# Sparse attention and FP4 feed-forward on one core: the exponentials of a score pair split into two, each score bank signalled by itself

## The reference

```
h = layernorm(x) * (1 + ca) + sa
x = x + ga * attention(h)
h = layernorm(x) * (1 + cb) + sb
x = x + gb * ffn(h)          # fp4_linear(silu(fp4_linear(h, gate)) * fp4_linear(h, up), down)

# attention: 16 heads of 32 features, 4 sequences, so 64 heads in all
top_idx = top_k(norm(Q), 409)          # only the 409 longest queries of a head attend
scores  = Q[top_idx] @ K.T / sqrt(32)  # 409 x 2048
out[top_idx] = softmax(scores) @ V     # every other row is zero
return out @ Wo.T + bo
```

## Time and profile before

| | |
|---|---|
| median of 3 runs | 3447.15 us (3444.97 to 3452.52) |
| the profiled execution | 3417.03 us |
| its span, first to last instruction | 3415.1 us |
| mean granted clock of PE in it | 0.976 |
| busy: PE, PEld | 3216.7 us (94%), 1493.7 us (44%) |
| busy: DVE, POOL, ACT | 2582.2 us (76%), 1541.0 us (45%), 1109.4 us (32%) |
| scores (L1414), first to last start | 736.8 to 1670.2 us |

### The profile page before, as it was taken

How to read it: one execution, slowest core, us unless ns; L and a number is a source line. 1 busy time by engine, 2 the same in 40 slices (tenths; PEclk the granted TensorE clock), 3 DMA queues, 4 the chain that set the end, 5 groups by cost and what they waited for, 6 DMA issues and landing times.

```text
span 3415.1 us, 49956 instructions
## 1 busy us (share of the span) xinstructions
PE 3216.7 (94%) x16716; PEld 1493.7 (44%) x16716; DVE 2582.2 (76%) x3868; ACT 1109.4 (32%) x1538; POOL 1541.0 (45%) x1358
## 2 busy tenths in 40 slices
PE   7989989869999999999679999999999999999998
PEld 3544444423333333333235555555555555555554
DVE  4656758746666666666368989989998998999895
ACT  6751212226666666666311111111111111111111
POOL 4431222345565555555234444444445444444442
PEclk9999999979999999999889999999999999999999
DMA  6755448636333333232201110010011001001000
GB/s 225 251 185 157 128 127 251 179 85 210 104 86 109 91 94 114 81 82 81 92 19 32 31 31 28 31 31 31 28 34 31 28 31 31 31 28 34 31 19 16
DMA packets 203080, 282.19 MB, mean 83 GB/s; under 512 B 59508, under 2 KB 115188, under 8 KB 202228
## 3 DMA queue, kind: packets, MB, share of 16 engines
q1 hardware_dynamic: 186616, 274.42, 26.4%
q0 software_dynamic: 16384, 6.76, 1.1%
HBM read 169.36 MB, written 111.71 MB: 82 GB/s over the span
## 4 chain that ended last, share of the span: by engine, by line
PE 47%; DVE 1%; issue 1%; POOL 1%; DMA 0%; ACT 0%; SPq 0%; POOLq 0%; DVEq 0%
PE f_g L1924 4%; PE f_u L1924 4%; PE f_u L1923 4%; PE f_u L1925 4%; PE f_g L1925 4%; PE f_g L1923 4%; PE f_d L1946 4%; PE f_d L1947 4%; PE f_d L1945 4%; PE f_t L1935 2%; PE f_w L1902 2%; PE f_w L1903 2%; PE f_w L1904 2%; PE f_t L1911 1%; PE f_w L1896 1%
## 5 line engine op out<-in xcount | busy, mean ns | idle before, releaser
L1231 DVE TENSOR_REDUCE top<-ps_max 128x1 f32<-128x1024 f32 x384 | 463.2, 1222 | 232.6 <-PE ps_max L1376 231.7
L1319 ACT ACTIVATE p<-ps_exp,p_bias 128x820 f32<-128x820 f32 x512 | 482.9, 943 | 370.1 <-PE ps_exp L1414 364.5
L1195 POOL DMA_INDIRECT o_d<-o_rows,chosen x256 | 249.0, 973 | 344.8 <-DVE o_rows L1266 275.3
L1425 PE MATMUL ps_out<-p,v_tok 128*33 128x410 f32 x2048 | 403.2, 515 | 0.0
L1856 ACT ACTIVATE silu<-f_g 128x512 f32<-128x512 f32 (+1 forms) x192 | 107.8, 562 | 798.3 <-PE f_u L1925 798.3
L1414 PE MATMUL ps_exp<-q_exp,k_exp 98*128 98x410 f16 x1024 | 268.0, 344 | 43.6 <-ACT p L1319 43.5
L1174 POOL DMA_INDIRECT q_sel<-q_d,chosen x256 | 244.0, 953 | 79.6 <-issue 62.7
L1923 PE MATMUL f_g<-gu,xT_hi 128*128 128x512 f16 (+1 forms) x768 | 277.5, 361 | 1.0 <-DVE xT_lo L1661 1.0
L1924 PE MATMUL f_g<-gu,xT_hi 128*128 128x512 f16 (+1 forms) x768 | 277.5, 361 | 0.0
L1925 PE MATMUL f_g<-gu,xT_lo 128*128 128x512 f16 (+1 forms) x768 | 277.5, 361 | 0.0
L1924 PE MATMUL f_u<-gu,xT_hi 128*128 128x512 f16 (+1 forms) x768 | 277.5, 361 | 0.0
(11 more groups left out here) (241 smaller groups left out, 6609.8 us busy)
## 6 DMA issues: line engine op xcount, KB each, us to landing
k_max<-k_d SPq DMA_DIRECT2D x192, 128.0 KB, 3.0
k_exp<-k_d SPq DMA_DIRECT2D x192, 128.0 KB, 2.6
v_d<-v SPq DMA_DIRECT2D x16, 1056.0 KB, 9.4
v_tok<-v_d SPq DMA_DIRECT2D x64, 264.0 KB, 2.7
x<-in_x SPq DMA_DIRECT2D x16, 1024.0 KB, 9.1
q_d<-q SPq DMA_DIRECT2D x16, 1024.0 KB
a_in<-o_d SPq DMA_DIRECT2D x64, 256.0 KB, 2.6
f_x<-in_x SPq DMA_DIRECT2D x64, 256.0 KB, 2.6
```

Of the source, the lines that this page charges most:

```text
L1195: pool.indirect_dma_start(o_rows, bass.IndirectOffsetOnAxis(ap=con["chosen"][0:n, t, h:h + 1], axis=0), o_rows_of[u][0:n, t, :], None).the ...
L1231: ve.tensor_reduce(top[:, t, half:half + 1], ps[:, :, :].rearrange("p a n -> p (a n)"), AX.X, ALU.max, negate=True).then_inc(max_done, 1)
L1319: act.activation(p32[k % PB][:, :, :], ps_exp[:, :, 0:NQ], ACT.Exp, bias=con["p_bias"][:, 0:1], scale=scale).then_inc(p_done, 1)
L1425: last = pe.matmul(ps_out[at:at + VCOLS, 0:NQ], v_tok[u][:, t, :], p32[k % PB][:, s, :], start=k == 0, stop=k == STEPS - 1)
```

## The change

Every count of `s_ready` and `p_done` goes from one a step to two a step, one for each bank. `scores` waits, before each of its two matmuls, until the exponential of the same bank of the step before is done, and signals each matmul by itself. `exponentials` issues two instructions of 410 columns, each behind the signal of its own bank, and signals each by itself. `weigh` waits for both halves. The waits of SP, DVE and ACT at the head's end count accordingly and stand for the same events as before. No instruction is moved past another, and nothing outside these functions is touched.

```diff
@@ load_k_exp (SP), queries_again (DVE), take_top (ACT), each the same edit @@
-                    need(sp, s_ready, h * STEPS - STEPS)
+                    need(sp, s_ready, h * TILES - TILES)
...
@@ exponentials (ACT) @@
                 def exponentials(i, k):
-                    act.wait_ge(s_ready, i * STEPS + k + 1)
                     need(act, pv_done, i * STEPS + k - PB + 1)
-                    act.activation(p32[k % PB][:, :, :], ps_exp[:, :, 0:NQ], ACT.Exp, bias=con["p_bias"][:, 0:1],
-                                   scale=scale).then_inc(p_done, 1)
+                    for s in range(PER):
+                        act.wait_ge(s_ready, i * TILES + k * PER + s + 1)
+                        act.activation(p32[k % PB][:, s, :], ps_exp[:, s, 0:NQ], ACT.Exp, bias=con["p_bias"][:, 0:1],
+                                       scale=scale).then_inc(p_done, 1)
@@ scores (PE) @@
-                    need(pe, p_done, i * STEPS + k)
                     for s in range(PER):
-                        at = (k * PER + s) * P
-                        last = pe.matmul(ps_exp[:, s, 0:NQ], k_exp[u][:, at:at + P], q_exp[u][:, :], start=True, stop=True)
-                    last.then_inc(s_ready, 1)
+                        c = k * PER + s
+                        need(pe, p_done, i * TILES + c - PER + 1)
+                        pe.matmul(ps_exp[:, s, 0:NQ], k_exp[u][:, c * P:(c + 1) * P], q_exp[u][:, :], start=True, stop=True)\
+                          .then_inc(s_ready, 1)
@@ weigh (PE) @@
-                    pe.wait_ge(p_done, i * STEPS + k + 1)
+                    pe.wait_ge(p_done, i * TILES + k * PER + PER)
```

More of the change, by code:

```diff
@@ L1251, in queries_again @@
                     ve.wait_ge(qsel_done, h + 1)
-                    need(ve, s_ready, h * STEPS - STEPS)
+                    need(ve, s_ready, h * TILES - TILES)
                     ve.tensor_copy(q_exp[u][0:KROWS, :], q_max[u][:, :]).then_inc(qexp_done, 1)
@@ L1312, in take_top @@
                     act.wait_ge(rows_ready, h + 1)
-                    need(act, s_ready, h * STEPS - STEPS)
+                    need(act, s_ready, h * TILES - TILES)
                     act.activation(q_exp[u][KROWS:KROWS + 2, :], ps_misc[0:2, 0:NQ], ACT.Copy).then_inc(rows_done, 1)
                 def exponentials(i, k):
-                    act.wait_ge(s_ready, i * STEPS + k + 1)
                     need(act, pv_done, i * STEPS + k - PB + 1)
-                    act.activation(p32[k % PB][:, :, :], ps_exp[:, :, 0:NQ], ACT.Exp, bias=con["p_bias"][:, 0:1],
-                                   scale=scale).then_inc(p_done, 1)
+                    for s in range(PER):
+                        act.wait_ge(s_ready, i * TILES + k * PER + s + 1)
+                        act.activation(p32[k % PB][:, s, :], ps_exp[:, s, 0:NQ], ACT.Exp, bias=con["p_bias"][:, 0:1],
+                                       scale=scale).then_inc(p_done, 1)
                 def take_output(h):
```

## The result

| | before | changed |
|---|---|---|
| median of 6 runs each, side by side | 3449.8 us (3444.97 to 3453.74) | 3462.7 us (3460.21 to 3465.36) |
| ratio, with its 95% interval | | 1.0039 (1.0026 to 1.0052) |
| the profiled execution | 3417.03 us | 3460.89 us |
| scores, first to last start | 736.8 to 1670.2 us | 731.2 to 1713.3 us |

The change makes the kernel slower by 0.4%, 13 us. The forecast was 3401 us, faster by 46. The two profiled executions differ by 44 us, three times as much as the medians: the one that the prediction was made from is 33 us faster than the median of its own kernel, the changed one is 2 us faster than its own. The execution that the prediction was made from is also faster than every timed run of its kernel. That difference turned out to be half of the story.

A forecast was written before the change was run, and what follows sets the result against it. PE was taken to bound the attention stage; removing its 0.78 us a head of waits for ACT (43.5 to 49.1 us, taken as 46), with additions at nothing, brings the median from 3447.15 to 3401 us, range 3388 to 3420.

The forecast's parts named there:

- What bounds the kernel, and where PE waits: Attention stage: PE sets the pace, waiting 43.5 us for the exponential, seen before the scores of steps 3 and 7.
- The length of a half, and the distance of two: ACT's two exponentials per pair: each 0.50 us, starts 0.40 apart, so PE sees the second end at 1.34, at worst 1.52.
- All three losses go: PE's losses in steps 2, 4 and 6 of a head, 0.78 us together, vanish; at 1.52, 11 us of 49 stay.
- The loss of step 4: After four chunk matmuls PE would end at 1025.14 but starts scores at 1025.22: 0.08 us a head, to vanish.
- the 0.43 of step 2: PE is free at 1021.28 but starts the next pair at 1021.71: 0.43 us a head, to vanish.
- the 0.27 of step 6: After four small matmuls PE is free at 1028.80 but starts at 1029.07: 0.27 us a head, to vanish.
- the sum of 46: Whole kernel: 46 us saved, taken between 43.5 us of noted idle time and 49.1 from 0.78 us in 63 heads.
- rival 1: ACT's halves follow slowly, or PE's signals cost something, or both: saving 28 to 38 us, some 3414; chance 0.12.
- What the change adds on PE, priced at nothing: PE's 512 more waits, as many signals, and register instructions in the loop: taken as no added time.
- The trace that the sum was made from: Profiled execution of 3417.0 us: the same 46 us saving was carried to the runs' median, 3447.15 to 3401.
- Rival 3: Each pair's second matmul pays fully for its wait and signal: 61 us on PE, net +15, 3462; chance 0.05.
- Rival 2: The split does not shorten the loop, ACT beginning neither half before both scores exist: saving about 0, 3447; chance 0.05.

The follow-up runs named there:

- g1_pe_straight: The changed kernel with PE's part of the hardware loop alone written out as straight code: 3383.86 us, ratio 0.9927, beside a kernel before of 3409.8.
- set 2: Runs on one chip of changed and unchanged kernels with single engines' loops written out, and of the pair signal; kernel before 3409.8 us, no late starts in four profiles.
- set 5: Runs on one chip without indirect DMAs (both kernels) or without key and value loads (changed kernel); kernel before 3418.2 us.
- k1_no_indirect: The changed kernel, looped, with queries gathered for the first two heads only and no outputs scattered: 3368.4 us, ratio 0.9854.
- e4_signals: The kernel before, single exponential kept, PE signalling each of the two scores matmuls and ACT waiting for the second: 3457.39 us, ratio 1.0021.
- e1_same: The kernel before, unchanged, timed and profiled again: 3449.14 us, ratio 0.9997; profiled execution 3441.98 us.
- e5_pair_signal: The changed kernel, looped, but PE signals each pair of scores once; ACT's split and PE's wait for each bank stay: 3411.99 us, ratio 1.0005.
- e3_after_straight: The changed kernel with the hardware loop over 56 heads written out for all engines: 3400.42 us, ratio 0.9855.

## Why the prediction was wrong

**What bounds the kernel, and where PE waits.** Right. PE is the bound, and the waits in steps 3 and 7 are the ones that the split changes. The forecast for PE's waits for ACT, under 5 us, is even met in g1_pe_straight (3.3 us up to 1640), as the second matmul's wait lies inside its row. But the head was to take 13.8 us then, and takes 14.15.

**The length of a half, and the distance of two.** This step failed first: "Its length I take from the copies of 410 columns, 0.50" and "I take 0.40". An exponential of 410 columns takes 0.60, and two of them start 0.48 to 0.50 apart. The second half ends 1.48 behind the pair, not 1.28, and PE sees it at 1.54, not 1.34. The upper bound that the prediction worked out, 1.52, was even passed by 0.02. The copy is a different operation. The whole exponential of 820 columns (0.94) against 0.60 gives 0.34 us for 410 columns and 0.26 whatever the size; if a copy takes its columns at the same rate, an estimate, its 0.50 holds only 0.16 of the latter.

**"All three losses go."** The loss of step 4 went (1.56 to 1.48 from pair to pair). Of the 0.43 of step 2, 0.11 arrived; 0.14 shows first as the wait of the second matmul (1.54 against the 1.40 at which it could have started), and the other 0.18 is the hold by `take_output`, which the prediction checked for the exponential behind it, but not for the `weigh` that waits for `o_done`. It took that `weigh` step for cover ("behind it lies a `weigh` step with 1.95 us"), when the start of that step was the thing held. Its own times gave it away: the copy at 1.18, 0.51 long, and `weigh` 0.10 later is 1.79 behind the pair of step 2 against 2.09 before, so only 0.30 of the 0.43, with the halves as fast as it took them. Of the 0.27 of step 6, 0.20 arrived: from the pair of step 6 to the pair of step 0 is 3.51 us in the medians before and 3.32 after. With 0.04 from step 0, where every other head of before started its exponential late by a register instruction, the head is 0.43 shorter, 27 us in 63 heads. So where nothing starts late, the sum of 46 is 26.4 (set 2) to 28.5 (set 5). That is at the lower end of rival 1 (28 to 38), half for its reason and half by luck: halves that follow slowly are 11 us in its sum, the signals that it added cost nothing, and the 0.18 of `take_output`, another 11 us in 63 heads, is in none of the rivals.

**What the change adds on PE, priced at nothing.** Right where nothing starts late: the follower of a pair comes 0.36 behind it, in g1_pe_straight (1051.34 to 1051.70) as in the looped k1_no_indirect (0.36, median of steps 0, 2 and 6), so wait, register instruction and signal of the second matmul are free. The Trainium skill's rule (TensorE: Matmul & The Clock Gate, the per-tile semaphore tail, 26.3 ns for each increment) finds no place in that row. It is stated for matmuls side by side in the array, which these are not. With late starts the 512 signals of e4_signals leave some 3 us that its interval does not tell from nothing; the other 4.3 of its 7.7 us are a register instruction's on ACT.

**The trace that the sum was made from.** This step cost the sign. "Its own time lies 30 us below the median of the runs; with the same saving the median goes from 3447.15 to 3401 us": the saving was not the same, as the runs had late starts, which the profiled execution did not have. Its sum put them at nothing. The bill, from the table of heads: the kernel before loses 15.23 - 14.58 = 0.65 us a head to them, 36 us over 55 heads; the changed one 15.51 - 14.15 = 1.36, 75 us. The difference, 39 us, less the 27 of the split is 12, and 12.9 was measured between the medians. The stretch from the first scores to the last says the same: 969.4 us in e1_same, 982.1 in the changed kernel. In whole executions the 36 us don't show in full: e1_same's profiled one (3441.98) is 25 us longer than the first (3417.03), as the rest of the program took 11 us less in it, and no run shows why. Why the late starts cost the changed kernel twice as much stays open.

**The rivals.** Rival 3's time, 3462, is the measured one by accident. Its mechanism, a second matmul that is 0.10 late in every pair, does not exist: the second matmul starts 0.18 behind the first wherever its bank is free. Rival 2's time is that of e5_pair_signal, for half of its reason: ACT began neither half before both scores were there, because that kernel told it so late. None of the rivals had late starts; the profile shown had no trace of them but one, the 30 us, which the prediction named and carried over unchanged.

**A version that beats both.** e3_after_straight is 1.45% faster than the kernel before in a set with late starts, and g1_pe_straight 0.73% in one without.

## What to carry to other kernels

Where the profiled execution is clearly faster or slower than the median of the timed runs, that gap is a term of the sum: profile the kernel again until a profile lies among its timed runs, before the price of anything is read from it. When a two-bank instruction is split, take the fixed part from the same operation at two sizes, and follow each half to every engine that waits for it, the copy queued behind it included; a wait that vanishes from the table of waits may have moved into the length of a row or lost its name, so compare idle and busy time of the whole group. A hardware loop with late starts is worth one run written out.

## What the hardware showed beyond that

- In some sets of runs, and inside the hardware loop above all, PE's semaphore updates come late, in the changed kernel 1.1 us behind the end of their matmul (median of the 108 late starts), and ACT starts within 0.08 us of them. Writing out the loop removed 42 us of 3449.6 from the kernel before and changed nothing in a set without late starts (3410.27 against 3409.8, PE's loop alone).
- The same kernel has its median at 3410, 3418 or 3446 to 3450 us in different sets, with its runs within a set 4 to 14 us apart, and on one chip at 3446 and at 3418.
- A register instruction between a signal and the exponential costs 0.08 us (0.56 against 0.64 behind the pair, and e4_signals); the second of two exponentials of 410 columns starts 0.48 to 0.50 behind the first, 0.10 before its row is over.
